# One block of adaLN attention and experts on one core: the router's product ahead of the projection in two steps, the second mixing weights scaled beside the last product of batch one

## The reference, cut to what matters

```python
h = _layernorm(x) * (1 + ca) + sa
x_shift = einsum('btd,ed->bte', roll(h, -512), Wts) * g + h * (1 - g)
xn = layernorm(x_shift) * ln_w + ln_b
wkv = exp(-exp(time_first) * sigmoid(xn @ Wk.T)) * (xn @ Wv.T)
s_t = s_{t-1} * exp(time_decay) + wkv_t
x = x + ga * (s @ Wo.T)
h = _layernorm(x) * (1 + cb) + sb
x = x + gb * ffn(h)
```

## Time and profile before

| | |
|---|---|
| time, median of 3 runs | 775.45 us (769.95 to 778.86) |
| profiled execution | 778.62 us, span 776.8 us |
| mean granted clock of TensorE | 0.951 |
| TensorE busy | 704.5 us, 91% of the span |
| VectorE, ScalarE, GpSimd busy | 55%, 35%, 26% |
| moved by DMA | 111.45 MB, mean 143 GB/s |

### The profile page before, as it was taken

The page is one execution under the profiler, slowest core; times in us unless marked ns, Lnnn a source line. Parts: engine busy times, 40 slices in busy tenths (PEclk is TensorE's granted clock), DMA queues, the critical chain, the costliest instruction groups (busy, mean ns, idle before and its releaser), DMA issues.

```text
span 776.8 us, 9100 instructions
## 1 busy us (share of the span) xinstructions
PE 704.5 (91%) x3281; PEld 489.9 (63%) x3281; DVE 423.9 (55%) x780; ACT 268.8 (35%) x525; POOL 205.5 (26%) x202
## 2 busy tenths in 40 slices
PE   5988779999899778999899999999998999897995
PEld 3666547767587655878466556655655566775773
DVE  2748657488667695873403423314123135878877
ACT  2444774665645342112124132222231142322320
POOL 0154442534214120000000000000000004788881
PEclk9999986999959998999999999999999999998998
DMA  8560000000131003005578877878888772511111
GB/s 285 180 236 1 0 14 28 25 17 14 41 136 43 25 0 122 0 1 200 196 274 289 291 254 277 299 268 306 313 304 302 254 277 81 147 49 35 42 41 68
DMA packets 48152, 111.45 MB, mean 143 GB/s; under 512 B 9056, under 2 KB 13172, under 8 KB 48108
## 3 DMA queue, kind: packets, MB, share of 16 engines
q1 hardware_dynamic: 41708, 102.46, 37.1%
q0 software_dynamic: 6400, 8.42, 3.8%
HBM read 110.83 MB, written 12.58 MB: 159 GB/s over the span
## 4 chain that ended last, share of the span: by engine, by line
PE 35%; DMA 6%; DVE 4%; issue 4%; POOL 3%; SPq 1%; ACT 1%; POOLq 0%; DVEq 0%
PE bank L1555 13%; PE bank L1610 9%; PE bank L1567 6%; PE bank L1627 5%; DMA expert_rows<-ye 3%; DMA egu<-in_L_ffn_Wu_dram 2%; POOL egu L654 2%; DVE ytmp L1280 1%; DMA xg<-h_rows,slot_tok 1%; PE bank L1598 1%; POOL ed L654 1%; PE bank L1616 1%; PE bank L1660 0%; DVE prod L1148 0%; DVE prodL L1150 0%
## 5 line engine op out<-in xcount | busy, mean ns | idle before, releaser
L1555 PE MATMUL bank<-xsH,wguH 128*128 128x512 f32 x352 | 145.1, 412 | 7.1 <-DVE xsL L1140 4.2
L1555 PE MATMUL bank<-xsL,wguH 128*128 128x512 f32 x352 | 139.6, 397 | 0.0
L1555 PE MATMUL bank<-xsH,wguL 128*128 128x512 f32 x352 | 139.2, 395 | 0.0
L636 POOL DMA_INDIRECT xg<-h_rows,slot_tok x16 | 15.4, 964 | 311.8 <-PE bank L1598 239.3
L1555 PEld LDWEIGHTS bank<-xsH,wguH 128*128 128x128 f32 x352 | 67.6, 192 | 33.2 <-issue 15.3
L1567 PE MATMUL bank<-wdH,prodH 128*128 128x512 f32 x176 | 75.9, 431 | 12.7 <-DVE prodL L1150 7.7
L1610 PE MATMUL bank<-egu,xeT 128*64 128x352 f32 x512 | 82.2, 475 | 3.7 <-DMA egu<-in_L_ffn_Wu_dram 3.7
L1148 DVE TENSOR_TENSOR prod<-bank,silu 128x512 f32<-128x512 f32 x38 | 26.2, 690 | 100.0 <-PE bank L1555 78.1
L1555 PEld LDWEIGHTS bank<-xsL,wguH 128*128 128x128 f32 x352 | 67.2, 191 | 15.0
L1555 PEld LDWEIGHTS bank<-xsH,wguL 128*128 128x128 f32 x352 | 67.3, 191 | 13.1 <-issue 0.5
L1567 PE MATMUL bank<-wdL,prodH 128*128 128x512 f32 x176 | 71.2, 404 | 0.0
(11 more groups left out here) (229 smaller groups left out, 1120.4 us busy)
## 6 DMA issues: line engine op xcount, KB each, us to landing
egu<-in_L_ffn_Wg_dram SPq DMA_DIRECT2D x32, 704.0 KB
egu<-in_L_ffn_Wu_dram SPq DMA_DIRECT2D x32, 704.0 KB
ed<-in_L_ffn_Wd_dram SPq DMA_DIRECT2D x32, 512.0 KB, 5.5
h2T<-in_L_wmod_dram SPq DMA_DIRECT2D x6, 1024.0 KB, 8.2
ed<-in_L_ffn_Wd_dram SPq DMA_DIRECT2D x32, 192.0 KB, 6.6
xres<-in_L_attn_x_dram SPq DMA_DIRECT2D x4, 1024.0 KB, 10.6
h_rows<-ho SPq DMA_DIRECT2D x16, 256.0 KB, 2.0
expert_rows<-ye SPq DMA_DIRECT2D x16, 256.0 KB, 7.5
```

What stands on the lines that cost most here:

```text
L636: gp.indirect_dma_start(xg[:, :], None, h2_dram[:, :], bass.IndirectOffsetOnAxis(slot_tok[:, j:j + 1], axis=0)).then_inc(xg_in, 16)
L1555: ins = mm.matmul(bk[:, :], l[f][:, w, c, :], r[:, c, :], start=(k == 0), stop=(k == 3 * C - 1))
```

## The change

In steps 9 and 17 the projection of tile t - 5 goes to the end of PE's step, behind the router's product. The list `PRODUCTS` follows, so the two change places in the banks: in step 9 the router's product now takes the bank that the projection had. Product 10 uses the same bank next, so it now waits for the copy of the logits, where it waited for the residual sum of tile 4. On ACT the copy of the logits goes ahead of `norm_out(t - 5)`; the rest of the routing on ACT stays where it was. In step 17 the projection no longer stands between the two early pieces. Step 13 stays as it was.

The second mixing weights are scaled earlier in step 7: on ACT right behind the copy `hT` of tile 8, with a wait for each of the first three chunks until product 7 has read that chunk (new semaphore `w_read`, three increments by PE), and on DVE ahead of `mix_front(7)`.

The four scalings have moved ahead of nine other instructions. The diff:

```diff
--- before.py
+++ after.py
@@ -261,13 +261,13 @@
              "xhat_ok hi_ok lo_ok wr_zero s_full0 s_full1 s_taken0 s_taken1 mix_ok "
              "xn_ok ho_ok h2_ok h2_sent0 h2_sent1 h2_sent2 e_tanh e_fac st_ok "
              "vef_ok vex_ok veh_ok rsf_ok rsx_ok rsh_ok dve_self pool_self")
-        (w_in, sg_exp, rb_ok, shift_ok, ex_ok, pos_full, mask_ok, scan_ok, route_ok,
+        (w_in, w_read, sg_exp, rb_ok, shift_ok, ex_ok, pos_full, mask_ok, scan_ok, route_ok,
          picked_ok, ids_ok, at_ok, ones_ok, tok_full, tab_ok, slotw_ok, nb_ok, nbx_ok, nbh_ok, hn_ok, xrow_ok,
          whi_ok, wlo_ok, xhi_ok, xlo_ok, g_full, silu_ok, u_full,
          prod_ok, phi_ok, plo_ok, d_full0, d_full1, d_used0, d_used1, x_acc,
          xg_in, et_full, et_taken, eg_full, esilu_ok, eprod_ok, ey_full, ye_ok, ye_sent, ye_free,
          gu_in, dn_in, y_in0, y_in1, y_in2, y_used, y_first, y_read, y_sum, final_ok, out_done) = sems(
-             "w_in sg_exp rb_ok shift_ok ex_ok pos_full mask_ok scan_ok route_ok "
+             "w_in w_read sg_exp rb_ok shift_ok ex_ok pos_full mask_ok scan_ok route_ok "
              "picked_ok ids_ok at_ok ones_ok tok_full tab_ok slotw_ok nb_ok nbx_ok nbh_ok hn_ok xrow_ok "
              "whi_ok wlo_ok xhi_ok xlo_ok g_full silu_ok u_full "
              "prod_ok phi_ok plo_ok d_full0 d_full1 d_used0 d_used1 x_acc "
@@ -306,6 +306,7 @@
 
         STEPS = NT + 6
         FFN_FROM = 10
+        ROUTER_FIRST = (9, 17)
 
         def before_mixer(t):
             return [("h", t + 1)] if t + 1 < NT else []
@@ -341,9 +342,11 @@
                 LATE_TURN = len(TURNS)
             TURNS += before_mixer(t) + amid(t) + late(t)
             PRODUCTS += [("mixer", t)] if t < NT else []
+
+            PRODUCTS += [("router", router_group(t))] if t in ROUTER_FIRST else []
             PRODUCTS += [("project", t - 5)] if 0 <= t - 5 < NT else []
             PRODUCTS += [("kv", scan_group(t))] if scan_group(t) is not None else []
-            PRODUCTS += [("router", router_group(t))] if router_group(t) is not None else []
+            PRODUCTS += [("router", router_group(t))] if t not in ROUTER_FIRST and router_group(t) is not None else []
 
         turn_at, turns_in = {}, dict.fromkeys(T_BANKS, 0)
         for q, t in enumerate(TURNS):
@@ -751,10 +754,13 @@
                     a.activation(partial[:, n % 2, :], partb[n % 2][:, :], ACT.Copy).then_inc(part_ok, 1)
 
                 def scale_weights(b):
-                    if b:
-                        product_full(act, ("mixer", b * BT - 1))
                     act.wait_ge(sa_ok, 1)
                     for c in range(C):
+                        if b:
+                            if c < C - 1:
+                                act.wait_ge(w_read, c + 1)
+                            else:
+                                product_full(act, ("mixer", b * BT - 1))
                         a.activation(wtsH[:, c, :], wtsT[:, c, :], ACT.Copy, scale=dcol[:, b, K_1CA, c:c + 1]).then_inc(wts_hi, 1)
 
                 def decay_factor(g):
@@ -891,6 +897,8 @@
                     g, s = divmod(t - FFN_FROM, GT)
                     for q in before_mixer(t):
                         take(q)
+                    if t == BT - 1:
+                        scale_weights(1)
                     if g >= 0 and s in (1, 2):
                         prod_hi(0, g, s - 1)
                     if g >= 0 and s < 2:
@@ -901,8 +909,8 @@
                         take(q)
                     if t < NT:
                         norm_mixed(t)
-                    if t == BT - 1:
-                        scale_weights(1)
+                    if t in ROUTER_FIRST:
+                        logits_out(router_group(t))
                     if 0 <= t - 5 < NT:
                         norm_out(t - 5)
                     if g >= 0 and s == 2:
@@ -917,7 +925,8 @@
                     for q in late(t):
                         take(q)
                     if router_group(t) is not None:
-                        logits_out(router_group(t))
+                        if t not in ROUTER_FIRST:
+                            logits_out(router_group(t))
                         sigma_exp(router_group(t))
                         split_group(0, g + 1)
 
@@ -1506,6 +1515,8 @@
                         for l, r in ((hi, wtsH), (hi, wtsL), (lo, wtsH)):
                             ins = mm.matmul(s_bank[k][:, :], l[:, c, :], r[:, c, :], start=(n == 0), stop=(n == 3 * C - 1))
                             n += 1
+                        if t == BT - 1 and c < C - 1:
+                            ins.then_inc(w_read, 1)
                     ins.then_inc(s_full[k], 1)
 
                 def keys_values(g):
@@ -1687,8 +1698,8 @@
                     if t < NT:
                         mixer(t)
 
-                    new_states = t % GT == 1 and t > 9
-                    if 0 <= t - 5 < NT and not new_states:
+                    new_states = t == 13
+                    if 0 <= t - 5 < NT and not new_states and t not in ROUTER_FIRST:
                         project(t - 5)
                     if t < GT:
                         vector_product(t + 3)
@@ -1710,6 +1721,8 @@
                         turn(q)
                     if r is not None:
                         router(r, [2, 3])
+                    if t in ROUTER_FIRST:
+                        project(t - 5)
 
                 for u, (p, g) in enumerate(UNITS):
                     if u < EARLY:
```

## The result

The changed kernel takes **767.16 us** (median of 4 runs, 764.32 to 769.59); the kernel before, timed beside it, 777.15 us (4 runs, 769.95 to 778.95). The ratio is 0.9884, 95% interval [0.9845, 0.9922]. Later runs of both gave 767.09 us and 0.9892 [0.9854, 0.993].

What follows compares the result with a forecast made beforehand. TensorE (busy 91%) was taken as the bound, except in the reordered steps, where a chain through ACT, DVE and POOL ends last. +0.4 - 4.2 - 3.0 = -6.8 us from 775.45 gives 768.6 us (chance 0.45), range 762 to 778.

Steps and rivals of the forecast that it cites:

- Part 1: Step 7, weights scaled earlier: product 8 starts 1.9 us earlier, given back on ACT; +0.4 us, bounds -1.9 and +2.8.
- Part 2: Step 9, router ahead of projection: product 10 and group 0's half product start earlier; -4.2 us, bounds -6.9 and -1.0.
- Part 3: Step 17: wait for states removed, xsL of group 2 ends last; -3.0 us, bounds -5.1 and -0.4.
- B: Rival, steps 9 and 17: the gaps drop the clock briefly or not at all; 763.9 us, chance 0.17.
- C: Rival: the clock stays down longer, since two gaps remain; -1.0 us, 774.4 us, chance 0.20.
- D: Rival: keys/values 1, product 9 and router at half clock behind Part 1's gap; +1.8 us, 777.3 us, chance 0.10.
- E: Rival: the gain ends in a later wait that doesn't move, such as the experts' loads; 775.4 us, chance 0.08.
- Within 1%: Whole kernel: time between 767.7 and 783.2 us, within 7.8 us of no change; chance 0.57.

Runs made afterwards that it cites:

- rows_first: Changed kernel with ScalarE's two next_rows of step 7 moved ahead of the copy of the split gate weights; 766.79 us, 0.9906 of the kernel before.
- change_again: The changed kernel itself, unaltered, timed again beside other variants; 767.09 us, 0.9892 of the kernel before.
- router9: Kernel before with the router ahead of the projection in step 9 alone, weights not moved; 770.98 us, 0.9948.
- router17: Kernel before with the router ahead of the projection in step 17 alone, weights not moved; 771.15 us, 0.9955.
- weights_only: Kernel before with only the second mixing weights scaled earlier, router and projection where they were; 773.78 us, 0.9979.
- warm17: The change without the weights' move, 22 unread products put into TensorE's gap ahead of group 2's half product in step 17; 766.48 us, 0.9899.
- xs17: The change without the weights' move, group 2's xsH and xsL taken forward in ScalarE's and VectorE's queues in step 17; 764.53 us, 0.9882.
- pool_late: The change without the weights' move, GpSimd's rows of step 9 held until VectorE's four xsL subtractions are done; 766.29 us, 0.9905.
- best: The changed kernel with rows_first's move and the edits of xs_all; 760.21 us, 0.9798 of the kernel before.
- xs_all: xs17 with its edit in steps 9 and 21 too, and VectorE's last two split-weight subtractions moved from step 9 to 8; 760.05 us, 0.9826.

## Why the prediction was right, and where it was not

Times on the span of before:

| | before | forecast | after +2.8 |
|---|---|---|---|
| product 8 starts | 97.33 | 95.4 | 95.0 |
| states(1) start | 115.35 | 115.7 | 115.7 |
| product 10 starts | 128.84 | 122.5 | 122.3 |
| half product, group 0, starts | 133.74 | 129.3 | 128.1 |
| the same, ends | 136.60 | 132.4 | 132.8 |
| half product, group 2, starts | 225.89 | 218.9 | 218.8 |

The forecast of the last row is 222.7 less the 3.8 us of the first two parts; that of the row above it is 4.4 less 0.2 earlier than before.

**Part 1, +0.4 us.** Right in size: the states came 0.4 later, and neither comparison gives the weights' move a gain or a loss that can be told. **Wrong in mechanism:** "a gap ahead of keys/values 1, which waits for xnT(7)". The step that failed was to take the input in view for the only condition of those products: the gap ends with the bank of product 8 [rows_first]. Its size is wrong too, 4.56 us and not 2.3, and that is the clock, which the forecast left out here. Product 8 ran at half clock in before (97.33 to 102.72, 5.39 us) and at full clock in after (92.20 to 95.14, 2.94 us), so PE came to the gap 4.7 us earlier, 2.3 by the start and 2.4 by the clock. It cost nothing because the chain that sets the states runs on ACT, DVE and POOL and passes beside PE: in change_again keys/values 1 end at 111.28, and ACT comes to them at 112.64 without having waited.

**Part 2, -4.2 us.** The sum has a slip: part 2 counts from states that are already 0.35 later, so its -4.2 holds part 1, and the +0.4 is added a second time. By its own times the forecast is -4.2 at the end of the half product of group 0, and -7.2 in all. Measured are 136.60 - 132.8 = 3.8 in after and 4.5 in change_again; router9 alone gives 3.7. One profile is good to a few tenths only, so that 3.8 meets the -3.8 of the sum is luck. Two errors cancel besides. PE does not idle 2.4 us ahead of product 10 but 0.78 and 0.29. The projection starts at 119.1, not at 117.9, since it too waits for a bank, that of product 9 [0.78 <-DVE mx], and at half clock projection and transpose fill the rest; the start of product 10, set by ACT's copy of the logits, is as forecast. The half starts 1.2 earlier than forecast, for the clock returns during product 10 (123.40). And xsL's four chunks take 5.21 us against 2.5; in before, GpSimd's rows of that step were nearly over when they began. So the half waits twice inside, 1.2 us.

**Part 3, -3.0 us.** Measured: 230.54 - 220.21 - 2.8 = 7.5 at the end of the half product, less the 3.8 from step 9, is 3.7; change_again gives 7.4 less 4.5, 2.9; router17 alone 3.2. The wait for xsL is 5.63 us (5.3 forecast). What the forecast lacked is again the clock: it came back at 219.0, inside the half product, and not behind it. How much of the 3.7 is owed to the long half-clock stretch of before's own execution stays open; router17's median (0.9955) is what carries this part.

**The sum.** Forecast -6.8, shown in the profile at the end of the half product of group 2 -7.5. The pairs of medians give 0.9884 x 775.45 = 766.5 and 0.9892 x 775.45 = 767.1, so -8.4 to -9.0, and -6.8 (0.9912) lies inside both intervals. The profiled pair differs by more, 14.3, of which 2.8 lie ahead of step 7. Of the rest the profiled execution of before lost some in a half-clock stretch at 263.9 us that no variant shows there, weights_only, which gains nothing, among them; I read this as that execution's own, which was not shown otherwise.

**The rivals.** B, the clock holds: it fell in both steps, but for half as long, so a part of B's gain came. The Trainium skill (TensorE: Matmul & The Clock Gate, What's actually happening) puts the ramp's penalty under 1% of a typical kernel span. For one gap that fits what warm17 shows, 1.8 us of its span of 764.7. For the sum of a profile it doesn't: by the pages' granted clock some 0.049 x 776.8 us were lost in before and 0.036 x 762.5 in after, 38 and 27 us, before's slow start not counted, and the router's 6.88 against 3.66 us alone is nearly half the forecast. C, the clock stays down longer: the opposite was seen. D, slower: its condition came true, the gap was 4.56 us and keys/values ran at half clock (99.50 to 106.36), but product 9 started at 108.17 with the clock back, and the 1.6 us it lost were hidden. E, no effect: the -7.5 us of group 2's half product are kept to the end of the span.

**The chances.** "Within 1%" had 0.57, and the result, 1.16% below, lies just on the other side of that bound. The forecast was placed 0.9 us from it, so on which side the result would fall was open, though the time was met.

## What to carry to other kernels

When an in-order engine waits, move what is ready in front of the waiting work, and then ask of the next products which **bank** they write as well as which input they read. Price the move by the wait that stands behind it: here both steps ended at xsL, and taking xsL's producers forward in their queues brought, with rows_first's move, 6.9 us more, nearly as much again. An engine that is ahead of its inputs keeps little of a gain (of xs17's 5.6 us 2.5 were left); what counts is the chain that delivers them. And compare several profiled executions before reading a microsecond out of one: here the same step, with the same code, differed by 2.2 us through the clock.

## What the runs showed of the hardware

**VectorE and GpSimd slow each other down.** Timeline of after, step 9, GpSimd and then VectorE:

```profile
123.21 1.30 POOL L584 TENSOR_TENSOR mx<-xhat,bc 128x512 f32<-128x512 f32 x1 [2.09 <-ACT xhat L723]
124.59 1.61 POOL L588 TENSOR_TENSOR mx<-mx,bc 128x512 f32<-128x512 f32 x1
126.17 1.72 POOL L595 TENSOR_TENSOR ho<-ho,bc 128x512 f32<-128x512 f32 x1
```
```profile
123.83 5.21 DVE L1149 TENSOR_TENSOR xsL<-h2T,xsH 128x512 fp32r<-128x512 f32 x4 [0.78 <-ACT xsH L821]
```

The tile's durations (ns: min, median, max) over 100 to 225 us:

```profile
L1149 DVE TENSOR_TENSOR xsL<-h2T,xsH x12: 676/684/1768, 123.8 to 216.9; 128x512 fp32r<-128x512 f32 x12
```

A VectorE subtraction with both operands in SBUF takes 0.68 us alone and up to 1.77 beside GpSimd's; GpSimd's own, 1.26 alone, take 1.61 and 1.72. The Trainium skill (SBUF — State Buffer, Who interferes with whom) says that the port pair which VectorE shares with GpSimd is an exclusive lock, and that a VectorE instruction with two SBUF inputs contends with a GpSimd instruction that reads SBUF. The trace agrees: each of the three stretched chunks ends 0.55 us behind the end of one of GpSimd's instructions, and pool_late, which parts the two in time, brings 2.50 us for the four.

**The clock can fall without a gap**, at 209.6 us in best, with TensorE busy 12.55 of the 12.60 us ahead of it. In xs_all, with the same order there and 12.60 of 12.60 us busy, it held. What decides between the two is not shown.
